# A transformer block on one core: attention's prologue reordered, the weight split spread out, a third pair of PSUM banks for the first gates

## What is computed

```python
def attention(x):                       # 16 heads of 8 columns
    q, k, v = split(x @ W_qkv + b_qkv)
    scores = einsum('bihd,bjhd->bhij', q, k) / sqrt(8) + bias[clip(i - j + 128, 0, 256)]
    return softmax(scores) @ v @ W_out + b_out

def ffn(x):                             # 128 -> 512 -> 512 -> 512 -> 128, ternary weights
    h = silu((x @ w1.T) * s1) * ((x @ w2.T) * s2)
    h = gelu((h @ h1.T) * h1s)
    h = gelu((h @ h2.T) * h2s)
    return (h @ w3.T) * w3s

x = x + layernorm(attention(layernorm(x)))
x = x + layernorm(ffn(layernorm(x)))
```

## Time and profile before

| | us |
|---|---|
| median of three runs | 310.52 |
| the three runs | 310.52, 310.61, 310.03 |
| the profiled execution, own time | 310.07 |
| its span in the trace | 308.3 |
| PE busy | 278.4 (90%) |
| DVE busy | 218.0 (71%) |
| ACT busy | 205.6 (67%) |
| POOL busy | 102.4 (33%) |

### The profile page before, as it was taken

The page is one execution under the profiler, slowest core; times in us unless marked ns, Lnnn a source line. Parts: engine busy times, 40 slices in busy tenths (PEclk is TensorE's granted clock), DMA queues, the critical chain, the costliest instruction groups (busy, mean ns, idle before and its releaser), DMA issues.

```text
span 308.3 us, 5129 instructions
## 1 busy us (share of the span) xinstructions
PE 278.4 (90%) x1857; PEld 183.7 (60%) x1857; DVE 218.0 (71%) x443; ACT 205.6 (67%) x315; POOL 102.4 (33%) x107
## 2 busy tenths in 40 slices
PE   8999679989999999999995999876899999999991
PEld 8665444645555555555553555434687888888870
DVE  4673866788789989989788559872754763574486
ACT  1777546678786877785874465955646988697750
POOL 6533010100610603906996931011752110510111
PEclk9999958999999999999998579989999999999997
DMA  6997401534032153470321000000000000010012
GB/s 178 306 202 131 172 1 43 201 88 105 9 99 72 48 187 115 154 215 14 104 72 51 22 0 1 4 1 2 1 0 2 0 0 0 2 34 0 3 35 72
DMA packets 21356, 21.17 MB, mean 69 GB/s; under 512 B 3664, under 2 KB 18768, under 8 KB 21072
## 3 DMA queue, kind: packets, MB, share of 16 engines
q1 hardware_dynamic: 20432, 20.52, 23.1%
q10 hardware_dynamic: 896, 0.29, 0.4%
HBM read 14.90 MB, written 5.64 MB: 67 GB/s over the span
## 4 chain that ended last, share of the span: by engine, by line
PE 50%; DVE 22%; ACT 8%; POOL 8%; issue 5%; SPq 3%; DMA 2%; ACTq 1%; POOLq 0%; DVEq 0%
PE place L1421 9%; PE place L1422 9%; DVE mx L678 7%; PE place L1231 6%; PE pv L1281 6%; PE place L1257 3%; ACT ring L992 3%; PE place L1223 3%; DVE y_and_z L613 2%; DVE stats L602 2%; DVE place L685 2%; PE place L1182 2%; POOL w_hi L562 2%; POOL w_lo L554 2%; POOL xn L564 2%
## 5 line engine op out<-in xcount | busy, mean ns | idle before, releaser
L678 DVE TENSOR_REDUCE mx<-place 128x4 f32<-128x1024 f32 x64 | 78.1, 1221 | 19.0 <-PE place L1231 18.1
L511 POOL TENSOR_TENSOR rstd<-mv,mhalf 128x2 f32<-128x2 f32 (+1 forms) x26 | 20.9, 805 | 158.5 <-DVE mv L610 158.5
L992 ACT ACTIVATE ring<-place 128x1024 f32<-128x1024 f32 x64 | 65.5, 1025 | 10.0 <-PE place L1268 5.3
L999 ACT COPY place<-raw 128x1024 f32<-128x1024 f32 x37 | 37.8, 1020 | 18.8 <-DVE mx L678 18.8
L1231 PE MATMUL place<-room,identr 128*128 128x512 f32 x128 | 49.5, 469 | 0.0
L1421 PE MATMUL place<-room,w_hi 128*128 128x512 f32 (+1 forms) x116 | 44.6, 387 | 0.7 <-DVE room L807 0.7
L1422 PE MATMUL place<-room,w_hi 128*128 128x512 f32 (+1 forms) x116 | 44.0, 382 | 0.0
L1281 PE MATMUL pv<-ring,vx 128*9 128x256 f32 x512 | 37.0, 411 | 2.4 <-ACT ring L992 2.4
L1257 PE MATMUL place<-room 33*128 33x256 f32 x256 | 33.7, 345 | 3.3 <-DVE place L685 1.8
L807 DVE TENSOR_TENSOR room<-ring,room 128x512 fp32r<-128x512 f32 x32 | 21.4, 690 | 18.6 <-ACT room L1082 18.6
L1223 PE MATMUL place<-room 33*128 33x256 f32 x256 | 29.1, 305 | 4.6 <-ACT ring L992 2.1
(11 more groups left out here) (138 smaller groups left out, 441.7 us busy)
## 6 DMA issues: line engine op xcount, KB each, us to landing
raw<-ext SPq DMA_DIRECT2D x8, 384.0 KB, 5.7
room<-q_parts SPq DMA_DIRECT2D x48, 64.0 KB
room<-k_parts SPq DMA_DIRECT2D x48, 64.0 KB
w_lo<-h SPq DMA_DIRECT2D x2, 1024.0 KB, 5.1
q_parts<-w_hi SPq DMA_DIRECT2D x4, 256.0 KB, 3.1
k_parts<-w_hi SPq DMA_DIRECT2D x2, 512.0 KB, 3.5
xs<-x SPq DMA_DIRECT2D x3, 256.0 KB, 5.6
w_lo<-w SPq DMA_DIRECT2D x3, 256.0 KB, 2.7
```

The lines of the kernel that those rows point to most:

```text
L511: nc.gpsimd.tensor_tensor(rstd[:, at:at + width], mv[:, at:at + width, 1], mhalf[:, 0:width], ALU.pow).then_inc(rstd_set, 1)
L678: nc.vector.tensor_reduce(mx[:, s // RPAIRS, :, :, s % RPAIRS].rearrange("p i k -> p k i"), max_tile(b * PAIRS + s)[:, :, :].rearrange("p ...
L992: nc.scalar.activation(probs[:, s % PRING, :, :, :].rearrange("p k j n -> p (k j n)"), score_tile(b * PAIRS + s)[:, :, :].rearrange("p k n ...
L999: nc.scalar.copy(score_tile(i)[:, :, :].rearrange("p k (j n) -> p k j n", j=2), pair_windows(raw[:, :, :], i % PAIRS)).then_inc(bias_set, 1)
```

## The change

- **Start.** The three loads of the q/k weights and biases get a semaphore each. DVE waits for the first alone and POOL for the second; the scaling of the bias comes later. The second half of q's spread weights is copied by ACT. The moments of unit 1 come before the normalization of unit 0.
- **Prologue.** Moments and normalization of unit 3 move from behind the eight maxima to s = 2 and 3 among them, those of unit 2 by one place; `q_and_k_low(2, 0)` moves from s = 4 to s = 6, `q_and_k_low(2, 1)` from s = 5 to behind the maxima. ACT does `minus_max(0, 0)` and `q_and_k_high(2, 0)` inside the last rows. POOL does `inv_std` of unit 3 after table 5. SP loads tables 5 to 7 together, and sends both rows of the first maxima.
- **Blocks.** PE's extra work at s = 6 moves ahead of `max_scores`. `SPLIT_AT` goes from 4 + 3 pieces in blocks 4 and 5 to 3 + 3 + 1 in blocks 4, 5 and 6. In the last block `scores(7, 7)` and its bias come right after `scores(7, 6)`, ahead of `weighted(7, 2)`.
- **Blank products.** `weighted(7, g)` gets 2, 2, 2 and 6 products of zeros before its wait for the exponentials, and `ffn` six more before `gate(0, 3)`.
- **FFN.** A third pair of banks, (4, 5), for gate 2; gates 3 and on alternate between (0, 1) and (2, 3), and the layers' banks are renamed around it. ACT's load of the Silu table comes before the last `keep_weighted`.

```diff
-        GBANK = ((0, 1), (2, 3))
-        A1_BANK = ((4, 5, 6, 0), (1, 2, 3, 4), (6, 4, 5, 0), (1, 2, 3, 6))
-        A2_BANK = ((5, 6, 0, 1), (2, 3, 4, 5), (4, 5, 0, 1), (2, 3, 6, 4))
-        Y3_BANK, BACK_BANK = (5, 0), (1, 2)
+        A1_BANK = ((4, 5, 6, 2), (3, 0, 1, 4), (6, 4, 5, 2), (3, 0, 1, 6))
+        A2_BANK = ((5, 6, 2, 3), (0, 1, 4, 5), (4, 5, 2, 3), (0, 1, 6, 4))
+        Y3_BANK, BACK_BANK = (5, 2), (3, 0)
+        def gate_banks(c, k):
+            n = c * NK + k
+            return ((0, 1), (2, 3), (4, 5))[n if n < 3 else (n - 3) % 2]
...
-        SPLIT_AT = ((), (0,), (1,), (2, 3), (4, 5, 6, 7), (8, 9, 10), (), ())
+        SPLIT_AT = ((), (0,), (1,), (2, 3), (4, 5, 6), (7, 8, 9), (10,), ())
...
+        BLANKS = (2, 2, 2, 6, 6)
...
-            load_table(sp, 5)
+            for s in range(5, PAIRS):
+                load_table(sp, s)
...
             store_parts(1)
-            load_table(sp, 6)
             sp.wait_ge(parts_out[1], PARTS_OUT)
             row_dmas(1, 0, PAIRS, second_rows_in)
-            load_table(sp, 7)
             load_x(4)
+            send_mrow(sp, 0, 0)
             store_parts(2)
...
             for b in range(B):
-                if b > 0:
-                    send_mrow(sp, b, 1)
+                send_mrow(sp, b, 1)
...
             x_inv_std(0)
-            pool.wait_ge(qk_w_in, 48)
+            pool.wait_ge(qk_w_in[1], 16)
...
                 table_high(s)
+                if s == 5:
+                    x_inv_std(3)
...
-            x_inv_std(3)
             x_inv_std(4)
...
             x_moments(0)
-            dve.wait_ge(qk_w_in, 48)
+            dve.wait_ge(qk_w_in[0], 16)
             nc.vector.tensor_scalar(wq_sb[:, :], wq_sb[:, :], scale, None, ALU.mult).then_inc(bq_scaled, 1)
-            nc.vector.tensor_scalar(bq_sb[:, 0:1], bq_sb[:, 0:1], scale, None, ALU.mult).then_inc(bq_scaled, 1)
+            x_moments(1)
+            x_normalize(0)
             dve.wait_ge(row_zeros, 1)
             dve.wait_ge(bq_scaled, 1)
-            spread_weights(nc.vector.tensor_copy, 0)
-            x_normalize(0)
+            spread_weights(nc.vector.tensor_copy, 0, (0,))
...
-            x_moments(1)
+            x_normalize(1)
...
+            dve.wait_ge(qk_w_in[2], 16)
+            nc.vector.tensor_scalar(bq_sb[:, 0:1], bq_sb[:, 0:1], scale, None, ALU.mult).then_inc(bq_scaled, 1)
             nc.vector.tensor_copy(identr[:, :], ident[:, :]).then_inc(identr_set, 1)
-            x_normalize(1)
             x_moments(2)
             q_and_k_low(1, 0)
             q_and_k_low(1, 1)
-            x_normalize(2)
...
             for s in range(PAIRS):
                 maxima(0, s)
                 if s == 0:
+                    x_normalize(2)
                     keep_v(0)
                 if s == 1:
                     keep_v(1)
-                if s in (4, 5):
-                    q_and_k_low(2, s - 4)
+                if s == 2:
+                    x_moments(3)
+                if s == 3:
+                    x_normalize(3)
+                if s == 6:
+                    q_and_k_low(2, 0)
+            q_and_k_low(2, 1)
             keep_v(2)
-            x_moments(3)
-            x_normalize(3)
...
+            act.wait_ge(row_zeros, 1)
+            act.wait_ge(bq_scaled, 1)
+            spread_weights(nc.scalar.copy, 0, (1,))
             keep_xT(0)
...
-            for s in range(2, PAIRS):
+            for s in range(2, PAIRS - 2):
                 take(s)
                 keep_rows(s)
-                if s == 5:
-                    keep_xT(2)
...
+            keep_xT(2)
+            take(PAIRS - 2)
+            minus_max(0, 0)
+            keep_rows(PAIRS - 2)
+            take(PAIRS - 1)
             q_and_k_high(2, 0)
-            minus_max(0, 0)
-            send_mrow(act, 0, 0)
+            keep_rows(PAIRS - 1)
             q_and_k_high(2, 1)
...
-            keep_weighted(B - 1, GROUPS - 1)
-
             nc.scalar.activation(table_loaded[:, :], mhalf[:, 0:1], ACT.Silu)
+            keep_weighted(B - 1, GROUPS - 1)
...
+                if b * GROUPS + g > 0:
+                    pe.wait_ge(oT_set, b * GROUPS + g)
+                if b + 1 == B:
+                    stream(pv, blank, blank, BLANKS[g])
                 pe.wait_ge(exp_done, b * PAIRS + (2 * g + 2))
...
-                    scores(b, s)
+                    if more or s not in BY_PE:
+                        scores(b, s)
+                    if s == 6 and 1 <= b <= 4:
...
                     if more:
                         max_scores(b + 1, s)
                         max_bias(b + 1, s)
-                    if s in BY_PE:
+                    if s in BY_PE and more:
                         score_bias(b, s)
+                    if s + 1 in BY_PE and not more:
+                        scores(b, s + 1)
+                        score_bias(b, s + 1)
...
+                n = c * NK + k
                 if c == 3 and k < 2:
                     pe.wait_ge(a2_set, (4, 6)[k])
-                elif c * NK + k >= 2:
-                    pe.wait_ge(gate_set, c * NK + k - 1)
+                elif n in (3, 4):
+                    pe.wait_ge(gate_set, n - 2)
+                elif n > 4:
+                    pe.wait_ge(gate_set, n - 1)
...
-                free = (((None, 0), (None, 0), (None, 0), (gate_set, 11)),
+                free = (((gate_set, 3), (gate_set, 3), (None, 0), (gate_set, 11)),
...
                 whole(gate, 0, exact, (0, 1, 2))
                 norm_T(B - 2)
+                pe.wait_ge(oT_set, B * GROUPS)
+                stream(pv, blank, blank, BLANKS[GROUPS])
                 gate(0, 3, exact)
```

More of the change, by code:

```diff
@@ L212, in build @@
         ident_loaded = sem("ident_loaded")
-        qk_w_in = sem("qk_w_in")
+        qk_w_in = [sem(f"qk_w_in{i}") for i in range(3)]
         wv_in = sem("wv_in")
@@ L366, in wait_score_place, with spread_weights @@
                 eng.wait_ge(exp_done, i - 2)
-        def spread_weights(copy, i):
+        def spread_weights(copy, i, halves=range(2)):
             weights = (wq_sb, wk_sb)[i][:, :]
-            for half in range(2):
+            for half in halves:
                 src = bass.AP(tensor=weights.tensor, offset=weights.offset + half * PAIRS,
@@ L819, in gate_product @@
                 nc.vector.scalar_tensor_tensor(
-                    out=act_f[:, G_HALF[c], k, :], in0=bank[GBANK[k % 2][1]], scalar=hs[:, 1, k:k + 1],
+                    out=act_f[:, G_HALF[c], k, :], in0=bank[gate_banks(c, k)[1]], scalar=hs[:, 1, k:k + 1],
                     in1=gate[:, k % 2, :], op0=ALU.mult, op1=ALU.mult).then_inc(gate_set, 1)
@@ L915, in _ @@
         def _(act):
-            for dst, src in ((wq_sb, wq), (wk_sb, wk), (bq_sb, bqk)):
-                act.dma_start(dst[:, :], src).then_inc(qk_w_in, 16)
+            for i, (dst, src) in enumerate(((wq_sb, wq), (wk_sb, wk), (bq_sb, bqk))):
+                act.dma_start(dst[:, :], src).then_inc(qk_w_in[i], 16)
             act.dma_start(brows_sb[:, :, :].rearrange("p a s -> p (a s)"), brows).then_inc(brows_in, 16)
@@ L1025, in _ @@
                         minus_max(b, 1)
-                        if b == 0:
-                            send_mrow(act, 0, 1)
                     if b == 0:
@@ L1048, in _ @@
                         keep_zT(b - 1)
+            nc.scalar.activation(table_loaded[:, :], mhalf[:, 0:1], ACT.Silu)
             keep_weighted(B - 1, GROUPS - 1)
-            nc.scalar.activation(table_loaded[:, :], mhalf[:, 0:1], ACT.Silu)
             act.wait_ge(scales_in, 80)
@@ L1058, in gate_silu @@
                     act.wait_ge(gate_set, n - 1)
-                nc.scalar.activation(gate[:, k % 2, :], bank[GBANK[k % 2][0]], ACT.Silu,
+                nc.scalar.activation(gate[:, k % 2, :], bank[gate_banks(c, k)[0]], ACT.Silu,
                                      scale=hs[:, 0, k:k + 1]).then_inc(silu_done, 1)
@@ L1179, in row_products @@
                 for i in range(2):
-                    if s == 0:
-                        pe.wait_ge(row_w_set[i], 2)
+                    pe.wait_ge(row_w_set[i], 2)
                     last = mm(bank[s % 2][:, i * S:(i + 1) * S], row_w[:, i, s, :], xT_of[0], start=(i == 0), stop=False,
@@ L1341, in _ @@
                 for s in range(PAIRS):
-                    scores(b, s)
+                    if more or s not in BY_PE:
+                        scores(b, s)
+                    if s == 6 and 1 <= b <= 4:
+                        pe.wait_ge(mrow_set, b * RANGES + 3)
+                        if b == 1:
+                            x_T(4)
+                        if b == 2:
+                            pe.wait_ge(xT_set, 5)
+                        if b in (2, 3):
+                            q_and_k(4, b - 2)
+                        if b == 4:
+                            v(4)
                     if more:
@@ L1388, in _ @@
                             v(3)
-                    if s == 6 and 1 <= b <= 4:
-                        pe.wait_ge(mrow_set, b * RANGES + 3)
```

(22 more changed lines are left out.)

2 lines of the change are left out of this document (removed).

## The result

| | before | after |
|---|---|---|
| median of the runs, us | 310.45 | 291.32 |
| the runs | 310.03 to 310.61 | 290.85 to 292.18 |
| profiled execution, its span | 310.07, 308.3 | 292.18, 290.4 |
| granted clock, mean | 0.949 | 0.991 |

The ratio is 0.939, 95% interval 0.937 to 0.941: faster.

The account below looks back on a forecast made before the run. PE, 90% busy, was held by waits and low clock at four places: start, prologue's end, block 5, way into the FFN. Gains 8.4 + 7.7 + 2.1 = 18.2 us off 310.07 give 291.9, stated as 292.0; range 288.5 to 298.

Parts of the forecast that it names:

- start: Kernel's first loads: the wait for the biases goes; 0.85 us gained, bounds none to 3.47.
- low half's order: Prologue's end: maxima of pairs 5 and 6 go before unit 2's low half; `scores(0, 0)` gains 1.75 us.
- unit 3 and clock: Prologue: moments and normalization leave the chain, 3.64 us, and PE's clock no longer falls, 2.2 us.
- SP's chain: From `scores(0, 3)`'s end to `scores(1, 0)`: 13.26 us, unchanged, moving by the same 8.4 us.
- s = 6: PE's extra work ahead of `max_scores` in the blocks: nothing, between -0.4 and +0.6 us per block.
- weight split: Block 5: three pieces free POOL earlier; interval to block 6 28.32 to 20.6, gain 7.7 us, about 2 waiting, rest clock.
- block 6: Its added split piece slows the second normalization from 0.60 to 1.76 us; loss of 0.85 us.
- first blanks: Last block: the first two groups of two blank products lie on the path, at 0.14 us each; -0.55 us.
- last block: With `scores(7, 7)` moved ahead, the last weighted group starts 1.8 us earlier, 1.5 of it clock that no longer falls.
- gates: Way into FFN: gate 2 loses its 1.40 us wait; `layer1(0, 0)` 3.5 us earlier, 1.8 from the block before included.
- the second sequence's rows: Rival in the prologue: rows arrive late behind SP's tables, PE waits before `max_scores(1, 0)`; up to 4 us, 296; chance 0.08.
- The clock rival: The clock falls anyway at one of the places, costing 3 to 6.6 us: 295 to 298.5; chance 0.14.

Follow-up runs that it names:

- e5: Kernel after with unit 3's moments and normalization, and POOL's power for them, back behind the eight maxima; 297.52 us (297.10 to 298.06).
- e2: Kernel after with the old SPLIT_AT, so without the new weight split; 296.17 us (294.54 to 299.52).
- e7: Kernel after with gates 2, 3 and 4 waiting for the product of the gate two before, banks as changed; 293.08 us (292.32 to 293.54).
- e1: Kernel before with the new SPLIT_AT alone; 301.91 us (301.43 to 303.14).
- e8: Kernel after with both q_and_k_low of unit 2 back at s = 4 and 5 among the maxima; 295.19 us (292.89 to 298.28).
- ref_before: Kernel before, unchanged, run again as an experiment for a second trace; 307.22 us (304.32 to 310.23), profiled execution 304.85.
- e9: Kernel after with the split one block earlier, three pieces each in blocks 3, 4 and 5, none in block 6; 292.13 us (291.16 to 294.14).
- e4: Kernel after without the 18 blank products; 291.13 us (290.70 to 291.97).

## Why the prediction was right

It forecast 292.0, and 18.2 us off the path; the trace has 18.83 off the path, of which the output's tail returns 0.97. Its three main mechanisms are shown by runs that undo one thing each (e5, e2, e7). That the sum is so near is in part luck, as terms that it lacked or mis-sized cancel:

| step | forecast | measured |
|---|---|---|
| start | 0.85 | 0.29 at the first row product, 0.66 at `take` |
| low half's order | 1.75 | 1.3 to 1.7, of another cause |
| unit 3 and clock | 5.8 | 6.46, from `scores(0, 0)` to `scores(0, 3)` |
| SP's chain | 0 | 0.4, in the profiled pair of executions only |
| s = 6 | 0 | -0.9 over four blocks |
| weight split | 7.7 | 8.09 |
| block 6 | -0.85 | -0.55 from `scores(7, 1)` on (-1.09 at `scores(7, 0)`) |
| first blanks | -0.55 | -0.45 |
| last block | 1.8 | 2.15 |
| gates | 1.7 | 1.66 |
| tail | none | -0.97 |

- **Start.** The bounds (0 and 3.47) held, and the reason for the low end was right: DVE waits 1.15 us for unit 1 at 5.69. But no gain is shown at the first row product: with the old start it is at 8.47, 8.57 and 7.48 (e1), with the new one between 7.96 and 9.14. The landing of unit 1, from 5.05 to 6.65 us in the traces with the new start, moves by more than the whole term. No run undoes the start alone.
- **Low half.** The size held, the cause named did not: e8 gives `scores(0, 0)` the same distance with the old order. By the traces it is ACT's earlier high half. The new order of the low halves pays behind it, in the maxima and the clock.
- **Unit 3.** e5 shows it, and that nothing pays for it in its new place, though it lasts 3.75 us there instead of 1.12. The forecast called it covered by the rows' round; it was.
- **SP.** The chain from `load_rows` to `scores(1, 0)` was forecast unchanged at 13.26, with its DMA wait, and is 11.84, so that `scores(1, 0)` starts at 52.85 and not near 54.3. Before, one issue of a pair of row DMAs took 2.26 us; after, each takes 0.9. That is not shown to be the change: in changed kernels such an issue takes 2.18 (e5) and 2.26 us (e8) too, and in the other execution of before 1.63. Why it varies stays open. It mattered little: the shift is 9.89 at `scores(1, 0)` and 8.61 at the end of block 1, 0.23 of the difference being the next point, and the block takes 20.40 us in ref_before and 20.39 in e1 where this execution of before has 20.79.
- **s = 6.** "Nothing" was wrong by 0.23 us per block, inside the bounds given (-0.4 to +0.6).
- **Weight split.** POOL's power follows DVE's variance as forecast, 20.2 us for an interval against 20.6. "About 2 are waiting and the rest clock" held for this execution (3.24 less 1.06 us of waiting is 2.18); in the other profiled one the clock had 4.3 less.
- **Block 6.** 1.76 forecast, 1.74 measured for the normalization. The Trainium skill's rule (SBUF — State Buffer, "Who interferes with whom": the shared port pair is locked for a whole instruction) agrees with that row: in both kernels DVE's pair ends 0.08 us behind a POOL instruction of 1.27 to 1.29 us. But a DVE instruction that is 1.14 us longer costs 0.38 to 0.53 in the end (e9, e2), less than the -0.85 of the sum.
- **Blanks.** The price of 0.14 was read from rows of weight loads: three loads took 0.42 us, the three products beside them 0.60 (PE's own rows). The six before the last group take 0.93 us from start to start, 0.16 each. On the path all 18 cost 0.86 (e4), not 1.39, as part of them fills waits. They are a loss all the same, as e4 and e1 keep full clock without them.
- **Last block.** The 1.5 us of clock in this term are a fall that the unchanged kernel has in one of its two profiled executions and not in the other; only 0.6 us are shown to be the order's.
- **Gates.** 1.40 us of waiting is gone, 1.06 of it is the third pair's, and the waits at gates 5 and 6 were foreseen; one of them (0.66) is there.
- **Rivals.** The clock did not fall in after, the second sequence's rows were in time (no wait on PE before `max_scores(1, 0)`), and PE had no low clock in the FFN: 1.00 from 200 to 284 us. The clock rival was a real one, as e8 (292.89 to 298.28) and e9's 294.14 show.

## What to carry to other kernels

Look at what a background job on a slow engine stands in front of: POOL's fourth piece delayed a power of 0.7 us and cost 4 to 8 us in block 5; what is above 4 is clock that went down behind PE's wait. Where an engine waits, first move work that is already there into the gap; of the blank products none paid here. A longer instruction off the path costs what is left of it at the next wait, here a third to a half. Where the clock falls after waits, compare several executions before a saving is put down to an edit.

## What the runs showed that was not expected

The kernel before has two times, and the granted clock makes the difference. Of its 19 runs beside the third set nine are near 305 us (from 304.22) and ten near 310 (to 310.91); beside the first and second set, on other chips, three and seven of 11 are near 310. The waits stand in the same places in both profiled executions. In that of 310.07 us the clock is 0.50 from 37.9, 167.6 and 205.2 us on, for 10.2, 13.6 and 3.3 us. In that of 304.85 it is 0.50 from 43.0 on for 6.8 us and from 169.3 on for 3.4, and 1.00 from 175 to 299. So the third fall is missing and the other two are shorter by 3.4 and 10.2 us, 27 us of low clock against 10, and the spans differ by 5.2 us. Windows of the same stretch in ref_before and e1_split_alone, which differ by nothing before block 4:

```profile
43.00:53.50 10.50, 9.69 (x49) 4.41 (x50) 5.73 (x6) 5.60 (x8) 0.00 (x0) 0.67 0.04 12
```

```profile
43.00:53.50 10.50, 10.35 (x42) 4.67 (x44) 4.96 (x6) 4.94 (x7) 0.00 (x0) 0.51 0.06 17
```

(0.67 against 0.51, with about the same waits ahead: 1.51 and 1.75 us in one, 1.52 and 1.75 in the other.) So the gain of this change is 4.3% or 6.1%, by how often before shows each value (ratios 0.957 and 0.939), while after keeps one value, 290.85 to 292.38 in all its ten runs. Its longest PE wait from 9 us to the FFN is 1.06 us. What decides when the clock falls in a given execution was not found.

At the start, 28 blank products take 5.48 us in after and 6.31 before, although the row of clocks has full clock there. Read one by one, they start 0.213 us apart before, all 28; in after they do so until 5.3 us and from there on 0.12 apart. The traces hold no record of the clock ahead of 5.3 us (after) and 7.2 us (before), and the row shows 1.00 where there is none. So the engine's pace is little more than half up to the first record, and that row can't be trusted in the first microseconds.
